# A two-layer graph network on one core: no accumulator table, the output bias on TensorE, and the edges' q rows gathered by source node

## The reference

```python
q = (x @ Wq + bq).reshape(n, DH, H) * scaling
k = (x @ Wk + bk).reshape(n, DH, H)
v = (x @ Wv + bv).reshape(n, DH, H)
s = jnp.einsum('edh,edh->eh', q[row], k[col])
m = jax.ops.segment_max(s, row, num_segments=n)
e = jnp.exp(s - m[row])
z = jax.ops.segment_sum(e, row, num_segments=n)
a = e / z[row]
out = jax.ops.segment_sum(a[:, None, :] * v[col], row, num_segments=n)
return out.reshape(n, -1) @ Wo + bo
```

## Time and profile before

| | |
|---|---|
| median of 3 executions | 4630.94 us (4628.98 to 4632.83) |
| profiled execution, its own time | 4610.09 us |
| span of its profile | 4608.5 us |
| mean granted TensorE clock | 0.937 |
| TensorE busy | 3692.4 us (80%) |
| VectorE busy | 3715.9 us (81%) |
| ScalarE busy | 2582.1 us (56%) |
| GpSimd busy | 2474.5 us (54%) |
| DMA | 947.78 MB, mean 206 GB/s |

### The profile page before, as it was taken

How to read it: one execution, slowest core, us unless ns; L and a number is a source line. 1 busy time by engine, 2 the same in 40 slices (tenths; PEclk the granted TensorE clock), 3 DMA queues, 4 the chain that set the end, 5 groups by cost and what they waited for, 6 DMA issues and landing times. The chain is left out here.

```text
span 4608.5 us, 89468 instructions
## 1 busy us (share of the span) xinstructions
PE 3692.4 (80%) x22858; PEld 2874.4 (62%) x22858; DVE 3715.9 (81%) x10138; ACT 2582.1 (56%) x7493; POOL 2474.5 (54%) x1690
## 2 busy tenths in 40 slices
PE   4999996678666666665777777777758999999999
PEld 2555554566544444444666666666647999999898
DVE  7999996942378878786888888888868999999997
ACT  3666664567622222223455445544536888888887
POOL 1000001345567777777777777777735555555553
PEclk8999998999989999997888888888878999999999
DMA  2444444689834444445787778777846666666664
GB/s 91 156 158 155 156 158 154 250 320 355 309 67 77 76 77 77 77 75 188 278 287 276 282 281 287 276 281 281 286 187 223 233 241 237 234 235 231 232 236 147
DMA packets 293629, 947.78 MB, mean 206 GB/s; under 512 B 51513, under 2 KB 84665, under 8 KB 280966
## 3 DMA queue, kind: packets, MB, share of 16 engines
q1 hardware_dynamic: 173350, 677.00, 41.8%
q0 software_dynamic: 106048, 218.26, 17.1%
q10 hardware_dynamic: 14112, 51.39, 2.8%
HBM read 500.36 MB, written 497.59 MB: 217 GB/s over the span
## 5 line engine op out<-in xcount | busy, mean ns | idle before, releaser
L1861 ACT ACTIVATE e_acc<-e_acc,e_attention 128x32 f32<-128x32 f32 x3136 | 686.0, 309 | 31.6 <-DVE e_attention L1997 20.9
L1454 PE MATMUL c_qkv_ps<-w_qkv_hi,c_ht_hi 128*128 128x256 f16 x2352 | 684.8, 291 | 0.0
L1454 PE MATMUL c_qkv_ps<-w_qkv_lo,c_ht_hi 128*128 128x256 f16 x2352 | 682.2, 290 | 0.0
L1454 PE MATMUL c_qkv_ps<-w_qkv_hi,c_ht_lo 128*128 128x256 f16 x2352 | 679.2, 289 | 0.0
L1816 POOL DMA_INDIRECT e_kv<-kv_table,e_near x392 | 430.3, 1098 | 123.4 <-issue 102.4
L816 PE MATMUL mix_ps<-w_mix,hb 128*128 128x256 f32 x1568 | 380.0, 398 | 134.5 <-ACT hb L790 72.1
L991 POOL DMA_INDIRECT agg_table<-gcn_summed,gcn_goal x240 | 388.5, 1619 | 136.3 <-DVE gcn_keys L954 54.7
L1425 ACT ACTIVATE c_hn<-c_x,c_shift,c_rstd 128x256 f32<-128x256 f32 x392 | 203.3, 589 | 439.3 <-DVE c_shift L188 439.3
L816 PEld LDWEIGHTS mix_ps<-w_mix,hb 128*128 128x128 f32 x1568 | 302.0, 198 | 212.9 <-ACT hb L790 100.3
L1265 ACT ACTIVATE gcn_summed<-gcn_sum_ps 128x256 f32<-128x256 f32 x240 | 91.9, 383 | 585.5 <-PE gcn_sum_ps L1248 451.9
L1380 POOL TENSOR_TENSOR c_qk<-c_q,c_kv 128x1024 f32<-128x1024 f32 x98 | 231.1, 2358 | 328.3 <-DVE c_kv L1482 328.2
(11 more groups left out here) (325 smaller groups left out, 10751.0 us busy)
## 6 DMA issues: line engine op xcount, KB each, us to landing
kv_table<-c_kv SPq DMA_DIRECT2D x98, 1024.0 KB, 7.7
acc_table<-c_acc SPq DMA_DIRECT2D x98, 544.0 KB, 3.0
e_acc<-acc_table SPq DMA_DIRECT2D x98, 544.0 KB
h_table<-h POOLq DMA_DIRECT2D x98, 512.0 KB, 2.9
h<-h_table SPq DMA_DIRECT2D x98, 512.0 KB, 5.1
y_table<-y_out ACTq DMA_DIRECT2D x98, 512.0 KB, 5.2
agg_table<-agg_out POOLq DMA_DIRECT2D x98, 512.0 KB, 5.5
c_agg<-agg_table SPq DMA_DIRECT2D x98, 512.0 KB, 5.0
```

The source lines that it names most:

```text
L1454: last = nc.tensor.matmul(qkv_ps[n][:, j * D:(j + 1) * D], h[u][:, kc, j * P:(j + 1) * P], w[:, kc, n * D:(n + 1) * D], start=m == 0, stop ...
L1861: last = nc.scalar.activation(mine, mine, ACT.Copy, scale=attention[u][:, j, h, 0:1])
```

## The change

- `acc_table` goes. `state_table` keeps 8 peaks and 8 weights for each node (`STATE` = 16, 256 bytes a partition). The edge stage loads the own v from the right half of `kv_table` (`mine`, runs of 1 KB) in place of the own sums, and multiplies the own weight into the attention. ScalarE's own sums in the dense stage go.
- GpSimd's addition of `b_out` in the dense stage goes. x1 is stored from its own two buffers, and its next writing waits for that store. The bias is split into three bf16 parts, which stand on rows 0 to 2 of `b_out`, and enters the output product as one more bf16 product with a matrix of ones, four a tile.
- The one-hot product for q goes. `slot_ends` holds for each slot the row numbers of both ends; GpSimd gathers the q rows too, four more gathers a tile, and VectorE's `qk` becomes one operation with both inputs in SBUF. The six q buffers are cleared first as well.
- The overflow block works on v's mean in place of the sum: one tile (all, if there is overflow) is copied from `kv_table` to `agg_table` before its loop and back after it, and its loop has one more gather and scatter.

```diff
@@ dense stage, GpSimd
+                        hold(pool, x1_stored[u], i * 16)
                         hold(pool, hn_ready[u], i)
                         nc.gpsimd.tensor_tensor(x1[u][:, :, :], agg[w][:, :, :], xb[w][:, :, :], ALU.add).then_inc(x1_ready[u], 1)
-                        hold(pool, x1_ready[u], i + 1)
-                        nc.gpsimd.tensor_tensor(xb[w][:, :, :], x1[u][:, :, :], b_out[:, :].unsqueeze(1).to_broadcast([P, ROWS, D]),
-                                                ALU.add).then_inc(x1_biased, 1)
@@ dense stage, ScalarE
-                        for j in range(ROWS):
-                            last = nc.scalar.activation(acc[u][:, j, SUMS:WEIGHTS], kv[u][:, j, 1, :], ACT.Copy,
-                                                        scale=n_self[:, bass.ds(tile * ROWS + j, 1)])
-                        last.then_inc(own_ready, 1)
@@ overflow block, SyncE
+                tiles = sp.value_load(slow_tiles[0:1, 0:1], min_val=1, max_val=NT)
+                with sp.Fori(0, tiles) as i:
+                    first = (NT - 1 - i) * TILE
+                    sp.dma_start(agg_table[bass.ds(first, TILE), :].rearrange("(p r) d -> p r d", p=P),
+                                 kv_table[bass.ds(first, TILE), D:2 * D].rearrange("(p r) d -> p r d", p=P)).then_inc(copied, 16)
@@ edge stage, SyncE
-                        sp.dma_start(flat(acc[w][:, :, :]), row_block(acc_table, t)).then_inc(acc_loaded[w], 16)
-                        w, n = in_ring(at(-2), SHORT)
-                        wait_past(sp, q_ready, (t - SHORT) * 2 + 2)
-                        sp.dma_start(flat(q[w][:, :, :]), row_block(q_table, t)).then_inc(q_loaded[w], 16)
+                        sp.dma_start(mine[w][:, :, :], kv_table[bass.ds(t * TILE, TILE), D:2 * D].rearrange(
+                            "(p r) d -> p r d", p=P)).then_inc(mine_loaded[w], 16)
+                        sp.dma_start(flat(state[w][:, :, :]), row_block(state_table, t)).then_inc(state_loaded[w], 16)
@@ edge stage, GpSimd
-                pool.wait_ge(kv_cleared, RING)
+                pool.wait_ge(kv_cleared, 2 * RING)
...
+                        for j in range(ROWS):
+                            nc.gpsimd.indirect_dma_start(out=q[w][:, j, :], out_offset=None, in_=q_table,
+                                                         in_offset=bass.IndirectOffsetOnAxis(ap=near[w][:, 0, j:j + 1], axis=0),
+                                                         bounds_check=TAB - 1, oob_is_err=False).then_inc(q_landed[w], 16)
@@ edge stage, TensorE
+                        nc.tensor.matmul(out_ps[:, j, :], all_b[:, :], b_out[:, :], start=True, stop=False)
...
-                            for j in range(2):
-                                last = nc.tensor.matmul(q_ps[half][:, j, :], hot_t[s][:, half * 2 + j, :], q[s][:, half * 2 + j, :],
-                                                        start=True, stop=True)
@@ edge stage, VectorE
-                        for half in two:
-                            dve.wait_ge(q_ready, t * 2 + (half + 1))
-                            v.scalar_tensor_tensor(qk[:, half * 2:half * 2 + 2, :], q_ps[half][:, :, :], SCALE,
-                                                   kv[w][:, half * 2:half * 2 + 2, 0:D], ALU.mult, ALU.mult).then_inc(qk_ready, 1)
+                        dve.wait_ge(q_landed[w], n * 64 + 64)
+                        v.scalar_tensor_tensor(qk[:, :, :], q[w][:, :, :], SCALE, kv[w][:, :, 0:D], ALU.mult, ALU.mult).then_inc(qk_ready, 1)
```

More of the change, by code:

```diff
@@ L338, in build @@
             n_loads = 15 + H
+            b_out_n = sb("b_out_n", [P, D], where=part)
+            b_rest = sb("b_rest", [P, 2, D], where=part)
+            b_thirds = sb("b_thirds", [P, 3, D], BF16, where=part)
             with nc.Block() as block:
@@ L510, in _ @@
                         dve.wait_ge(stocked, 2 * g + 2)
+                    left = b_out_n[:, :]
+                    for third in range(3):
+                        link(v.tensor_copy(b_thirds[:, third, :], left))
+                        if third < 2:
+                            link(v.tensor_tensor(b_rest[:, third, :], left, b_thirds[:, third, :], ALU.subtract))
+                            left = b_rest[:, third, :]
+                    link(v.tensor_scalar(b_out[:, :], b_thirds[:, 0, :], ident[:, 0:1], None, ALU.mult))
+                    for third in (1, 2):
+                        link(v.scalar_tensor_tensor(b_out[:, :], b_thirds[:, third, :], ident[:, third:third + 1], b_out[:, :], ALU.mult, ALU.add))
                     dve.wait_ge(w_peaks_ready, 1)
@@ L557, in build @@
             h1 = [sb(f"h1_{u}", [P, KC, TILE], where=part) for u in two]
-            zero = sb("zero", [P, 2 * WIDE], where=part)
+            zero = sb("zero", [P, 2 * D], where=part)
             third = HIST // 2
@@ L1149, in build @@
             own_degree = sb("sort_own_degree", [P, subtiles], where=part)
+            first_node = sb("sort_first_node", [P, NT, ROWS], where=part)
+            near_f = sb("sort_near_f", [P, subtiles], where=part)
+            first_ready = sem("sort_first_ready")
             over_ready = sem("sort_over_ready")
@@ L1227, in _ @@
                 v.tensor_copy(slow_cols[:, :], over[:, 1:2])
+                v.tensor_scalar(slow_tiles[:, :], slow[:, :], float(NT - 1), 1.0, ALU.mult, ALU.add)
                 for l in range(LAYERS):
@@ L1291, in build @@
             masked = [sb(f"c_masked{u}", [P, ROWS, H], where=part) for u in two]
-            acc = [sb(f"c_acc{u}", [P, ROWS, WIDE], where=part) for u in two]
+            state = [sb(f"c_state{u}", [P, ROWS, STATE], where=part) for u in two]
             has_self = sb("has_self", [P, NT * ROWS], where=part)
@@ L1298, in build @@
             x1_ready = [sem(f"c_x1_ready{u}") for u in two]
-            x1_biased = sem("c_x1_biased")
-            x1_stored = [sem(f"c_x1_stored{w}") for w in range(4)]
+            x1_stored = [sem(f"c_x1_stored{u}") for u in two]
             stats_ready = [sem(f"c_stats_ready{u}") for u in two]
@@ L1316, in build @@
             peak_ready = sem("c_peak_ready")
-            own_ready = sem("c_own_ready")
-            acc_stored = [sem(f"c_acc_stored{u}") for u in two]
+            state_stored = [sem(f"c_state_stored{u}") for u in two]
             c_chain = sem("c_chain")
@@ L1573, in load_columns, with _ @@
                 return eng.value_load(slow_cols[0:1, 0:1], min_val=1, max_val=most_cols)
+            @block.sync
+            def _(sp):
+                tiles = sp.value_load(slow_tiles[0:1, 0:1], min_val=1, max_val=NT)
[3 more added lines that the diff above has]
+                                 kv_table[bass.ds(first, TILE), D:2 * D].rearrange("(p r) d -> p r d", p=P)).then_inc(copied, 16)
+                columns = load_columns(sp)
+                hold(sp, column_free, columns + 1)
+                with sp.Fori(0, tiles) as i:
+                    first = (NT - 1 - i) * TILE
+                    sp.dma_start(kv_table[bass.ds(first, TILE), D:2 * D].rearrange("(p r) d -> p r d", p=P),
+                                 agg_table[bass.ds(first, TILE), :].rearrange("(p r) d -> p r d", p=P)).then_inc(copied, 16)
+                hold(sp, copied, tiles * 32)
             @block.gpsimd
@@ L1577, in _ @@
                 columns = load_columns(pool)
-                pool.memset(row_new[:, :], 0.0).then_inc(column_free, 1)
+                tiles = pool.value_load(slow_tiles[0:1, 0:1], min_val=1, max_val=NT)
+                hold(pool, copied, tiles * 16)
+                pool.memset(mean_new[:, :], 0.0).then_inc(column_free, 1)
                 with pool.Fori(0, columns) as n:
@@ L1699, in build @@
             kv = [sb(f"e_kv{w}", [P, ROWS, 2 * D], where=part) for w in long]
-            acc = [sb(f"e_acc{w}", [P, ROWS, WIDE], where=part) for w in long]
-            q = [sb(f"e_q{w}", [P, ROWS, D], where=part) for w in short]
+            mine = [sb(f"e_mine{w}", [P, ROWS, D], where=part) for w in long]
+            state = [sb(f"e_state{w}", [P, ROWS, STATE], where=part) for w in long]
+            q = [sb(f"e_q{w}", [P, ROWS, D], where=part) for w in long]
             x1 = [sb(f"e_x1_{w}", [P, ROWS, D], where=part) for w in long]
-            near = [sb(f"e_near{w}", [P, ROWS], I32, where=part) for w in long]
+            near = [sb(f"e_near{w}", [P, 2, ROWS], I32, where=part) for w in long]
             hot_h = [sb(f"e_hot_h{w}", [P, ROWS, P], F16, where=part) for w in short]
@@ L1715, in build @@
             below = [sb(f"e_below{u}", [P, ROWS, H, LAYERS + 1], where=part) for u in two]
-            weight = [sb(f"e_weight{u}", [P, ROWS, H, LAYERS + 2], where=part) for u in two]
+            weight = [sb(f"e_weight{u}", [P, ROWS, H, LAYERS + 1], where=part) for u in two]
             total = [sb(f"e_total{u}", [P, ROWS, H], where=part) for u in two]
@@ L1724, in build @@
             prefix_ps = part.enter_context(nc.psum_tensor("e_prefix_ps", [P, ROWS, P], F32))
```

(1 more changed line is left out.)

162 lines of the change are left out of this document (91 added, 71 removed).

## The result

| | before | after |
|---|---|---|
| median, 4 runs each | 4631.9 us (4629.0 to 4638.6) | 4821.6 us (4820.0 to 4825.5) |
| ratio, 95% interval | | 1.041 (1.039 to 1.043) |
| span of the profiled run | 4608.5 us | 4820.7 us |
| granted clock, whole span | 0.94 | 0.91 |

The change costs 190 us by the medians, beyond the upper end of the forecast. One plain fact is needed for all that follows: the chips were met in two conditions. In some measurements the kernel before takes 4597 to 4598 us (condition A), in others 4632 to 4645 us (condition B); two chips were met in both.

What follows compares the result with a forecast made beforehand. TensorE was taken to pace the edge stage, a closed loop of GpSimd and VectorE the dense stage. Dense -169, overflow block +18, preparation +5 and edge +198 give +52 us on 4630.9: 4683 us, range 4597 to 4768.

Steps and rivals of the forecast that it cites:

- Dense stage, -169 us: Dense stage: without GpSimd's `b_out` add VectorE's copy costs 0.18 instead of 2.10 us, 88 x 1.92 = -169 us.
- GpSimd chain: Dense stage: GpSimd's three operations, then VectorE's copy, shift, q and k, summed to a period of 11.2 us a tile.
- Rival (3): Dense stage: gain halves to -85 us because something else is held once the copy is free; 4767 us, chance 0.15.
- Own sums, 0 us: Dense stage: dropping four ScalarE operations a tile and 512 of 544 KB of store gains 0 us.
- Overflow block and first gather, +18 and +7.6 us: Before the edge loop: two serial table copies, one gather and one scatter, +18 us; six more memsets, +7.6 us.
- Fill, +23 us to the first multiply: Edge stage start: 20 more gathers at 1.31 us each before the first multiply, +23 us from the first gather.
- rival (2): Edge stage: GpSimd's gather issue is partly hidden or cheaper, near 1.0 us, period 10.4 us; 4421 us, chance 0.04.
- Edge stage, GpSimd, 13.1 us a tile: Edge stage: four more gathers use up GpSimd's 3.7 us idle, making it the bound at 13.1 us; tiles +167 us.
- the prediction's own sign of being wrong: Edge stage: the prediction is wrong if GpSimd's multiply still waits for VectorE for microseconds.
- Rival (4): Edge stage: idle TensorE falls to 1.2 GHz, period 13.9 us, +74 us more, 4757 us; chance 0.15.
- Rival (1): Both stages: dense gain (-200 us, 11.0 us a tile) exceeds edge loss (+151, 12.6 us); 4597 us, chance 0.13.

Runs made afterwards that it cites:

- dense_add: `onehot` with a third GpSimd add of 1024 elements, result unread, put back in the dense stage; 1.011 to the kernel before, in A.
- own_sums: `onehot` with the four ScalarE operations of the own sums put back in the dense stage, unread; 0.972 to the kernel before, in A.
- onehot: The changed kernel with the one-hot q product and the loads of q kept, so only the table and bias changes; 4461.5 us, 0.971, in A.
- qgather: The kernel before with the q gathers alone added; 4794.6 us, 1.043, in A.
- filler_again: The changed kernel with four unread TensorE products a tile ahead of the maxima's scores; 4823.5 us, 1.038, in B.
- hot_early: The changed kernel with the next tile's `hot_h` issued ahead of VectorE's wait for the edge products; 0.995 to the kernel before, in A.
- after_again: The changed kernel as it is, measured again in A; 4614.6 us, 1.0037 to the kernel before.

## Why the prediction was wrong

- **Dense stage, -169 us:** right, -172.9, and by the mechanism named. The copy is at 0.18 us and the loop at 11.3, and `dense_add` brings both back (+186 us). The terms of the GpSimd chain add up to 11.45 us and not to the 11.2 that stand behind them; the loop lies between. Rival (3), half the gain, is out.
- **Own sums, 0 us:** right (`own_sums`).
- **Overflow block and first gather, +18 and +7.6 us:** together +15.2. `onehot`, which has the block's copies and not the six further memsets, takes 63.5 us there: +9.3 for the block, +5.9 for the memsets. The price of a whole store's time to landing for each copy was too high.
- **Fill, +23 us to the first multiply:** right, +23.7. Gathers go at 1.31 us (1.01 busy, 0.30 between), so rival (2) is out. But the earlier trace rows held a sign that was read over. The 3.14 us of idle time before the first multiply there are a wait for `part_of`, and its `of_edge` waits for a semaphore that rises at 3492.91, though the record of the edge products ends at 3489.71. In `onehot`, in A, with the same 20 gathers, `of_edge` starts 0.04 us behind the products and the multiply at once behind the last gather. First the kernel before, then `onehot`:

```profile
3492.93 0.42 DVE L2016 TENSOR_TENSOR e_of_edge<-e_small_ps,e_layer 128x256 f32<-128x256 f32 x1 [2.05 <-remote]
```

```profile
3314.69 0.42 DVE L2073 TENSOR_TENSOR e_of_edge<-e_small_ps,e_layer 128x256 f32<-128x256 f32 x1
```

- **Edge stage, GpSimd, 13.1 us a tile:** the step that failed, in its sentence "That idle time is used up". It took GpSimd's 3.7 us behind the last gather for slack that four more gathers would fill, with `part_of` arriving meanwhile. In A that is so: 12.87 us with the change, 13.07 in `qgather`, and the whole change 1.0037 (the sum had 1.011). In B `part_of` does not arrive during gathers. The wait is still 2.4 us behind eight of them, which is the prediction's own sign of being wrong (a multiply that waits for VectorE for microseconds), and 97 tiles cost 351 us instead of 167. Those 184 us are the miss. The kernel before shows no such hold in its steady tiles: its four gathers end some 2 us ahead of the products, and `of_edge` follows the products' record within 1 us. Why results are held in B stays open.
- **Rival (4), the clock:** its sign was there (0.85 against 0.99, products at 1.91 us), its effect was not. In `filler_again` the granted clock of the stage is 0.96 and the tile 14.93 us. So the low clock does not make the 15 us.
- **Rival (1), a faster kernel:** not met by this change in either condition (1.041 and 1.0037). `hot_early`, another kernel, comes to 0.995 in A, with 12.4 and 11.3 us against the rival's 12.6 and 11.0.

The Trainium skill (GPSIMD Engine Reference, Key points), which the forecast drew on for VectorE's held operations, agrees with `dense_add`'s 2.20 us copy. That TensorE's results wait for a run of gathers is shown only by the rows above.

## What to carry to other kernels

An engine's wait behind its own run of gathers is not slack that more gathers may fill until a trace shows the awaited result arriving during gathers; here it did in one condition of the chip and not in the other, 12.9 or 15.0 us a tile. Compare an experiment only with the changed kernel measured beside it, however well the ratio to the kernel before seems to carry over: this study built a theory of the clock on such a comparison and had to give it up. The part of the change that pays, dropping GpSimd's add and the accumulator table, stands alone: 0.971, and 0.968 with `hot_h` issued early (measured in A only).

## What the hardware showed that was not expected

Condition B is visible before the loop is running, and in stages that the change does not touch. Count the semaphores that rise 0.2 to 8 us behind the recorded end of the operation that raises them. Between 1000 and 2100 us, mostly the convolution over the edges, where GpSimd gathers and scatters, there are 620 to 740 of some 5070 in each of the eight traces in B (623 in the kernel before), and at most 6 in each of the twelve in A; in the dense stage, without gathers, there is none in any of the twenty. (Some of these may be a record that the trace lost, so that the next rise is counted; that `of_edge` starts late does not rest on them.) The profile's page shows it as a wait of ScalarE that is not all put down to TensorE, in the kernel before and in `onehot` (A):

```profile
L1265 ACT ACTIVATE gcn_summed<-gcn_sum_ps 128x256 f32<-128x256 f32 x240 | 91.9, 383 | 585.5 <-PE gcn_sum_ps L1248 451.9
L1295 ACT ACTIVATE gcn_summed<-gcn_sum_ps 128x256 f32<-128x256 f32 x240 | 92.2, 384 | 583.4 <-PE gcn_sum_ps L1278 583.4
```

In the fill of the edge stage, while GpSimd issues 40 gathers, ScalarE does 21 of its 32 short operations in a row and then mostly one each 1.40 us, waiting for nothing that the profile shows; in the result's trace:

```profile
3326.78 4.56 ACT L1915 ACTIVATE e_mine<-e_mine,e_attention 128x32 f32<-128x32 f32 x21 [3.25 <-issue]
...
3333.13 0.32 ACT L1915 ACTIVATE e_mine<-e_mine,e_attention 128x32 f32<-128x32 f32 x1 [1.08 <-issue]
3334.53 0.32 ACT L1915 ACTIVATE e_mine<-e_mine,e_attention 128x32 f32<-128x32 f32 x1 [1.08 <-issue]
```

and in `after_again`, in A:

```profile
3330.65 6.89 ACT L1915 ACTIVATE e_mine<-e_mine,e_attention 128x32 f32<-128x32 f32 x32 [5.59 <-DVE e_attention L2043]
```

`filler_again` shows the same 21 and 1.40 us. The 32 operations wait for no other engine between one and the next, and neither do TensorE's unread products. In the tile of `filler_again` shown above they start 0.22 us apart at first, and then, from the last gather (4005.65 to 4006.66) until `of_edge` starts, up to 0.72 us apart:

```profile
4006.41 0.38 PE L1976 MATMUL e_idle_ps<-w_out,ident 128*128 128x256 f32 x1 [0.17 <-issue]
4007.13 0.38 PE L1976 MATMUL e_idle_ps<-w_out,ident 128*128 128x256 f32 x1 [0.34 <-issue]
```

So it is not only what passes between engines that is late during gathers in B, but also the start of operations that wait for nothing. The gathers are not slower (40 in 52.2 us in B, 54.0 in `after_again`), and the dense stage is the same (11.34 us a tile in both). What the condition is, and whether late starts and late semaphores have one cause, stays open. Also open is how `onehot` fares in B. Four gathers a tile end 3.1 us ahead of its `of_edge` in A, and in the kernel before, in B, 2.8 us, with the tile at 11.3 us, so little should be held; but it was not measured. Nor is there a trace of the kernel before in A, which would show where its 34 to 47 us between the conditions lie.
